# Attention B of a hybrid block: two small scalings moved from VectorE to ScalarE, and the next group's weight chunk converted later in the step

## The chip, the cores and the metric

One core of one Trainium2 chip runs the whole kernel. The metric is the device time in microseconds. The kernel before was timed three times: 1567.02, 1569.10 and 1569.83, median 1569.1.

## The reference, cut to what matters

The block computes attention A (32 heads of 16, 8 key groups, not causal), a mixture feed-forward, attention B, and the same feed-forward again, over 1024 tokens of width 512. Attention B is the part that matters here:

```
q, k, v = x @ w_q, x @ w_k, x @ w_v        # w = (4-bit integer - 8) * scale per 128 rows
q, k    = rope(q), rope(k)                 # 32 query heads, 8 key/value heads, head width 128
scores  = q @ k.T / sqrt(128), causal
attn    = softmax(scores)
out     = (attn @ v) @ w_o
```

## The kernel before, in words

Attention B runs over 8 groups g (one key/value head and R = 4 query heads each) and, in each, over T = 8 tiles t of 128 tokens: 64 steps, u = 8 g + t. In a step head h has scores of 128 queries against n = 128 (t + 1) keys, so that steps grow with t. All products are made of fp16 halves (high and low), three matmuls for each product.

Each engine has its own program, and within an engine everything runs in the written order; semaphores tie the engines together. There is no planner: the order around the change is the order in the function `step` of each engine.

TensorE (L1519): keys of head 0, the projection of the next tile (L1438), keys of head 1, half of the output product of the tile two before, keys of head 2, the other half, keys of head 3, then `turn_b` (L1453: five transposes of the next tile's rotated q and k) and `values` (L1500: attention times v for the tile before). Keys of head 0 wait for the low halves of the turned q and k (`s_ql`) and for the third exponentials of the tile before; keys of head 2 and 3 wait for exponentials 0 and 1 (`s_eb`), whose banks they write. `turn_b` waits for the rotation on GpSimd (`s_rpa`) and for the low half of v (`s_vl`). `values` waits for the transposing DMAs of the tile before (`s_tp`).

VectorE (L1066): `low` of heads 2 and 3 of the tile before (L1036, it writes the low half of the normalised attention), with `maximum` of head 0 between them; `dequantise` of one weight chunk of the next group (L932: tiles 0 to 3 have one of 768 columns, tiles 4 to 7 one of 512); the rotation of the next tile (L999, L1010); maximum 1; `invert` for heads 0 and 1; the low half of v (L992); maximum 2; low of head 0; maximum 3; `turned` (L1041, low halves of q, then k); low of head 1; invert for heads 2 and 3; `add` (L1051); `context_low` (L1059). `maximum` reduces a head's scores to the negated row maximum `nmr` (L1021) and multiplies it by the group's factor into `nmb` (L1023). `invert` scales the row sums `den` (L1031) and takes the reciprocal (L1034) into `rden`.

ScalarE (L659): `exponentials` of head 0 and 1 (L672, with the row sum in `den`, which a second instruction reads out of the accumulator), `values` (L638, high half of v), `high` of head 0 and 1 (L680: attention times `rden`, high half), `high_part` (L596: the dequantised chunk copied to fp16, L600 or L602), `turned` (L643: high halves of q, L645, and k, L648), exponentials 2 and 3, `context_high` of the tile before (L651), high 2 and 3. The last group has no chunk to dequantise or copy.

GpSimd (L511): `rope_add` (L500) and `low_part` (L502: what the fp16 copy left out, L505 or L508). The SyncE queue (L447): the DMAs of the chunk three steps on, which wait for earlier dequantised and split chunks, and a transposing DMA for each head (L459), which waits for `low`.

Quoted, a part of ScalarE's step (L683 to L698):

```
                exponentials(0)
                exponentials(1)
                if not end:
                    values(u + 1, par if t < T - 1 else 1 - par, t2)
                high(0)
                high(1)
                if not last:
                    high_part(g + 1, t, 1 - par)
                if not end:
                    turned(u + 1, t2, par if t < T - 1 else 1 - par)
                exponentials(2)
                exponentials(3)
                if exists(*before(g, t, 1)):
                    context_high(*before(g, t, 1))
                high(2)
                high(3)
```

Of the kernel before, what the change touches and what calls it, by code (L numbers as in the profile page):

```python
# [7 lines left out]
P = 128  # L8
# [9 lines left out]
R = NH // G  # L18
# [62 lines left out]
def build(nc, x_d, wq_d, bq_d, wk_d, bk_d, wv_d, bv_d, wo_d, bo_d,  # L81
# [6 lines left out]
    with ExitStack() as ctx:  # L88
# [67 lines left out]
        with ExitStack() as mem:  # L156
            xTh, xTl = (scoped(mem, f"xT{c}", [P, KC, S], F16) for c in "hl")
            qTh, qTl = (scoped(mem, f"qT{c}", [P, 2, R, P], F16) for c in "hl")
            kTh, kTl = (scoped(mem, f"kT{c}", [P, S + P], F16) for c in "hl")
            vh, vl = (scoped(mem, f"v{c}", [P, T + 2, P], F16) for c in "hl")  # L160
            cTh, cTl = (scoped(mem, f"cT{c}", [P, R, P], F16) for c in "hl")
            nmr = scoped(mem, "nmr", [P, R])
            nmb = scoped(mem, "nmb", [P, R])
            den = scoped(mem, "den", [P, R])
            rden = scoped(mem, "rden", [P, R])
            scoped(mem, "gap", [P, P])
            wh, wl = (scoped(mem, f"w{c}", [P, 2, KC, BW], F16) for c in "hl")
            woh, wol = (scoped(mem, f"wo{c}", [P, 2, R, D], F16) for c in "hl")
            st = scoped(mem, "st", [P, STAGES, BW])
            scale = scoped(mem, "scale", [P, 2, BW])  # L170
            cos = scoped(mem, "cosines", [P, T, HALF_D])
            sin = scoped(mem, "sines", [P, T, HALF_D])
            mask = scoped(mem, "mask", [P, P], BF16)
            ftmp = scoped(mem, "ftmp", [P, 4 * D + 16 * T + 8 * P + 4 * NE])
            hl = scoped(mem, "hl", [P, R, 2 * S], F16)
            hlT0 = scoped(mem, "hlT0", [P, R, 2 * (T - 1), P], F16)
            hlT1 = scoped(mem, "hlT1", [P, R, 2 * T, P], F16)
# [166 lines left out]
        def exists(g, t):  # L344

            return not (isinstance(g, int) and g < 0)
# [179 lines left out]
        def _(act):  # L526
# [132 lines left out]
            def step(g, t, par):  # L659

                u = g * T + t
                n = (t + 1) * P
                last = isinstance(g, int) and g == G - 1
                end = last and t == T - 1
                g2, t2 = after(g, t)

                def exponentials(h):
                    if exists(*before(g, t, 1)) is False:
                        act.wait_ge(s_nat[h], 64)
                        act.wait_ge(s_xh, 2 * T + 2 * h + 2)  # L670
                    act.wait_ge(s_nb, u * R + h + 1)
                    nc.scalar.activation(pr[:, h, 0:n], flat(2 * (h % 2), n), ACT.Exp, bias=nmb[:, h:h + 1],  # L672
                                         scale=factor[:, par, 0:1], accum_out=den[:, h:h + 1]).then_inc(s_eb, 1)

                def high(h):
                    if h % 2 == 0:
                        act.wait_ge(s_rd, u * 2 + h // 2 + 1)
                    if exists(*before(g, t, 1)):
                        act.wait_ge(s_tp[h], u * 16)
                    nc.scalar.activation(hl[:, h, 0:n], pr[:, h, 0:n], ACT.Copy,  # L680
                                         scale=rden[:, h:h + 1]).then_inc(s_hi, 1)

                exponentials(0)  # L683
                exponentials(1)
                if not end:
                    values(u + 1, par if t < T - 1 else 1 - par, t2)
                high(0)
                high(1)
                if not last:
                    high_part(g + 1, t, 1 - par)  # L690
                if not end:
                    turned(u + 1, t2, par if t < T - 1 else 1 - par)
                exponentials(2)
                exponentials(3)
                if exists(*before(g, t, 1)):
                    context_high(*before(g, t, 1))
                high(2)
                high(3)  # L698
# [21 lines left out]
        def _(dve):  # L720
# [295 lines left out]
                                               ALU.mult, ALU.mult).then_inc(s_rope, 1)  # L1016
                nc.vector.tensor_tensor(o[:, :, HALF_D:], rotary_in()[:, :, 0:HALF_D], sn, ALU.mult).then_inc(s_rope, 1)  # L1017

            def maximum(u, h, n, par):
                dve.wait_ge(s_sc, u * R + h + 1)  # L1020
                nc.vector.tensor_reduce(nmr[:, h:h + 1], flat(2 * (h % 2), n), AX.X, ALU.max, negate=True).then_inc(s_mxb, 1)  # L1021
                dve.wait_ge(s_mxb, u * R + h + 1)
                nc.vector.tensor_scalar(nmb[:, h:h + 1], nmr[:, h:h + 1], factor[:, par, 0:1], None,  # L1023
                                        ALU.mult).then_inc(s_nb, 1)

            def group_factor(g, par):
                nc.vector.tensor_copy(factor[:, par, :], factors[:, ds(g, 1), :].rearrange("p o a -> p (o a)")).then_inc(s_fcr, 1)

            def invert(u, a):
                dve.wait_ge(s_eb, u * R + 2 * a + 2)  # L1030
                nc.vector.tensor_scalar(rden[:, 2 * a:2 * a + 2], den[:, 2 * a:2 * a + 2], 1.0 / PSCALE, None,  # L1031
                                        ALU.mult).then_inc(s_dn, 1)
                dve.wait_ge(s_dn, u * 2 + a + 1)
                nc.vector.reciprocal(rden[:, 2 * a:2 * a + 2], rden[:, 2 * a:2 * a + 2]).then_inc(s_rd, 1)  # L1034

            def low(u, h, n):  # L1036
                dve.wait_ge(s_hi, u * R + h + 1)
# [28 lines left out]
            def step(g, t, par):  # L1066

                u = g * T + t
                n = (t + 1) * P
                last = isinstance(g, int) and g == G - 1  # L1070
                end = last and t == T - 1
                g2, t2 = after(g, t)
                one, two = before(g, t, 1), before(g, t, 2)
                if exists(*one):
                    low(u - 1, 2, (one[1] + 1) * P)
                if t == 0:
                    dve.wait_ge(s_fcr, g + 1)
                maximum(u, 0, n, par)
                if exists(*one):
                    low(u - 1, 3, (one[1] + 1) * P)  # L1080
                if not last:
                    dequantise(g + 1, t)
                if not end:
                    rope_cos(u + 1, t2)
                    rope_sin(t2)
                maximum(u, 1, n, par)
                invert(u, 0)
                if not end:
                    values_low(u + 1, par if t < T - 1 else 1 - par, t2)
                maximum(u, 2, n, par)  # L1090
                low(u, 0, n)
                maximum(u, 3, n, par)
                if not end:
                    turned(u + 1, t2, par if t < T - 1 else 1 - par)
                else:
                    final_statistics(0, 1)
                low(u, 1, n)
                invert(u, 1)
                if exists(*two):
                    add(u - 2, two[1], par if t >= 2 else 1 - par)  # L1100
                if exists(*one):
                    context_low(*one)
                if t == T - 1 and not last:
                    group_factor(g + 1, 1 - par)
# [482 lines left out]
```

## Time and profile before

| | |
|---|---|
| median of three runs | 1569.1 us |
| the profiled execution's own time | 1571.05 us |
| its span | 1569.2 us |
| TensorE clock over the span | 0.97 of full speed |
| steps of attention B | from 614 us to 1514 us of the span, 64 of them |
| instructions | 23528 |

The span is the time from the first to the last instruction of the program. Times of events are microseconds from the span's start. A row of the timeline gives start, duration, engine, line, operation and what is written from what; brackets at its end give how long the engine stood idle before it and whom it then waited for. TensorE's rows show start times well, but its ends are modelled. A row that groups instructions gives their count, their busy time, the mean of one in ns, and the idle time before them with its releasers.

### The profile page before, as it was taken

Reading aid. Unit: us, or ns where it says so; the run is one execution under the profiler, and the core shown is the slowest. Engines: PE = TensorE matmul, PEld = TensorE weight load, DVE = VectorE, ACT = ScalarE, POOL = GpSimd, SP = SyncE. Lnnn points to the kernel's source line nnn. Section 1 sums busy time; section 2 is a strip of 40 time slices with the busy share of each in tenths; the row PEclk is TensorE's granted clock in tenths of the full one; section 3 lists DMA queues with packets and bytes.
Section 4 is the critical chain, followed back from the end, with each engine's and each line's share of the span. In section 5 each row is a group of like instructions: output and inputs, shape, how many; then the busy total and the mean of one; then the engine's idle time right before and its main releaser. Section 6 shows DMA issues by size and latency. Waiting matters only on the chain.

```text
span 1569.2 us, 23528 instructions
## 1 busy us (share of the span) xinstructions
PE 1469.0 (94%) x7932; PEld 698.8 (45%) x7932; DVE 1237.7 (79%) x2583; ACT 868.9 (55%) x1468; POOL 237.6 (15%) x174
## 2 busy tenths in 40 slices
PE   5779999999999997899999999998999999999988
PEld 3412333333333354455555555554555555555534
DVE  4288888888886388787897887887887888878873
ACT  2205767676778324565665665664665665646630
POOL 2002000000000132221212212212212212211020
PEclk9957999999999998999999999999999999999989
DMA  3894000000000233566576575675684674653621
GB/s 97 150 143 134 1 1 0 0 0 0 0 0 11 64 94 98 105 140 144 121 137 139 120 150 127 129 147 120 128 160 111 141 145 110 134 96 67 115 54 54
DMA packets 352234, 144.64 MB, mean 92 GB/s; under 512 B 314680, under 2 KB 324408, under 8 KB 352128
## 3 DMA queue, kind: packets, MB, share of 16 engines
q1 hardware_dynamic: 352144, 143.48, 43.8%
q8 instruction: 52, 0.85, 0.2%
q14 instruction: 38, 0.31, 0.1%
HBM read 59.64 MB, written 6.19 MB: 42 GB/s over the span
## 4 chain that ended last, share of the span: by engine, by line
PE 73%; DVE 14%; ACT 6%; DMA 3%; issue 3%; SPq 0%; POOL 0%; DVEq 0%; ACTq 0%
PE ps L1433 9%; PE ps L1215 9%; PE ps L1435 9%; PE ps L1434 9%; PE ps L1268 7%; PE ps L1254 7%; PE ps L1395 4%; PE ps L1514 3%; PE ps L1516 3%; PE ps L1515 3%; ACT hl L680 2%; DVE hl L1038 2%; PE ps L1358 2%; DMA scratch<-pieces 2%; PE ps L1458 2%
## 5 line engine op out<-in xcount | busy, mean ns | idle before, releaser
L672 ACT ACTIVATE x<-ps,nmb,factor 128x128 f32<-128x128 f32 (+7 forms) x256 | 211.6, 832 | 290.9 <-DVE nmb L1023 290.9
L823 DVE TENSOR_REDUCE mx<-ps 128x1 f32<-128x512 f32 x512 | 326.4, 686 | 52.8 <-PE ps L1215 49.4
L581 ACT ACTIVATE proj<-ps 128x1024 f32<-128x1024 f32 x256 | 248.4, 1021 | 105.7 <-PE ps L1254 104.8
L1215 PE MATMUL ps<-ks,qs 96*128 (+1 forms) x512 | 200.1, 414 | 16.3 <-DVE mx L823 8.5
L1038 DVE SCALAR_TENSOR_TENSOR hl<-x,rden,hl 128x128 f16<-128x128 f32 (+7 forms) x256 | 208.3, 814 | 4.6 <-ACT hl L680 4.3
L680 ACT ACTIVATE hl<-x,rden 128x128 f16<-128x128 f32 (+7 forms) x256 | 184.1, 767 | 23.2 <-DVE rden L1034 22.5
L1021 DVE TENSOR_REDUCE nmr<-ps 128x1 f32<-128x128 f32 (+7 forms) x256 | 191.9, 750 | 0.0
L500 POOL TENSOR_TENSOR tmp<-tmp 128x640 f32<-128x640 f32 x64 | 98.4, 1538 | 532.1 <-DVE tmp L1017 532.1
L1433 PE MATMUL ps<-wh,xTh 128*128 128x256 f16 (+1 forms) x512 | 167.6, 327 | 0.0
L1434 PE MATMUL ps<-wl,xTh 128*128 128x256 f16 (+1 forms) x512 | 167.5, 327 | 0.0
L1435 PE MATMUL ps<-wh,xTl 128*128 128x256 f16 (+1 forms) x512 | 167.4, 327 | 0.0
L1433 PE MATMUL ps<-kTh,qTh 128*128 128x512 f16 (+3 forms) x384 | 125.8, 328 | 35.5 <-DVE kTl L1048 22.9
L1254 PE MATMUL ps<-qs,ks 99*128 (+1 forms) x512 | 153.0, 384 | 1.1 <-ACT proj L581 0.8
L1268 PE MATMUL ps<-proj,vcur 128*32 128x512 f32 x1024 | 137.2, 608 | 0.6 <-ACT proj L581 0.6
L1215 PEld LDWEIGHTS ps<-ks,qs 96*128 (+1 forms) x512 | 45.1, 97 | 192.8 <-DVE mx L823 138.3
L1434 PE MATMUL ps<-kTl,qTh 128*128 128x512 f16 (+3 forms) x384 | 125.5, 327 | 0.0
L1435 PE MATMUL ps<-kTh,qTl 128*128 128x512 f16 (+3 forms) x384 | 124.5, 326 | 0.0
L1514 PE MATMUL ps<-hlT,vh 128*128 128x512 f16 x288 | 110.5, 384 | 7.4 <-DMA hlT<-hl 6.9
L1516 PE MATMUL ps<-hlT,vh 128*128 128x512 f16 x288 | 110.4, 383 | 0.0
L1515 PE MATMUL ps<-hlT,vl 128*128 128x512 f16 x288 | 110.4, 383 | 0.0
L1433 PE MATMUL ps<-woh,cTh 128*128 128x512 f16 x256 | 97.5, 381 | 2.0 <-DVE cTl L1062 2.0
L1435 PE MATMUL ps<-woh,cTl 128*128 128x512 f16 x256 | 97.8, 382 | 0.0
(155 smaller groups left out, 2149.6 us busy)
## 6 DMA issues: line engine op xcount, KB each, us to landing
scale<-sp_n SPq DMA_DIRECT2D x32, 384.0 KB, 4.3
st<-in_L_attn_b_qw_q_dram SPq DMA_DIRECT2D x32, 256.0 KB, 2.8
st<-in_L_attn_b_qw_o_dram SPq DMA_DIRECT2D x32, 256.0 KB, 3.0
scale<-so_n SPq DMA_DIRECT2D x32, 256.0 KB, 3.6
qs<-scratch SPq DMA_DIRECT2D x24, 256.0 KB, 8.4
hlT<-hl SPq DMA_TRANSPOSE x256, 3.5
scratch<-pieces SPq DMA_DIRECT2D x5, 768.0 KB, 13.4
xnat<-attn_a_hidden_state_dram SPq DMA_DIRECT2D x8, 256.0 KB, 4.8
```

What stands on the lines that cost most here:

```text
L581: nc.scalar.activation(pbuf[:, e % 4, :].rearrange("p (b n) -> p b n", b=2), ps[:, b:b + 2, :], ACT.Exp, scale=float(HD) ** -0.5).then_inc ...
L672: nc.scalar.activation(pr[:, h, 0:n], flat(2 * (h % 2), n), ACT.Exp, bias=nmb[:, h:h + 1], scale=factor[:, par, 0:1], accum_out=den[:, h:h ...
L680: nc.scalar.activation(hl[:, h, 0:n], pr[:, h, 0:n], ACT.Copy, scale=rden[:, h:h + 1]).then_inc(s_hi, 1)
L823: nc.vector.tensor_reduce(mx[:, f, k // 2, k % 2:k % 2 + 1], ps[:, bank(k), :], AX.X, ALU.max).then_inc(s_mx, 1)
L1021: nc.vector.tensor_reduce(nmr[:, h:h + 1], flat(2 * (h % 2), n), AX.X, ALU.max, negate=True).then_inc(s_mxb, 1)
L1038: nc.vector.scalar_tensor_tensor(hl[:, h, n:2 * n], pr[:, h, 0:n], rden[:, h:h + 1], hl[:, h, 0:n], ALU.mult, ALU.subtract).then_inc(s_lo, 1)
L1215: mm(ps[:, bank, :], qs[0:STACK, ds(g * R + h, 1), f * HALF + qt * P:f * HALF + (qt + 1) * P], ks[0:STACK, ds(g, 1), kh * HALF:(kh + 1) * ...
L1254: ins = mm(ps[:, 4 + 2 * r + j, :], ks[0:STACK + NEG, ds(g, 1), kt * P:(kt + 1) * P], qs[0:STACK + NEG, ds(g * R + 2 * r + j, 1), f * HALF ...
L1268: ins = mm(ps[VW * j:VW * j + VW, 3, :], vcur[:, kt, :], pbuf[:, 2 * (kt % 2) + j // 2, (j % 2) * HALF:(j % 2 + 1) * HALF], start=(kt == 0 ...
L1433: mm(out, lh, rh, start=(start and i == 0), stop=False)
L1434: mm(out, lh, rl, start=False, stop=False)
L1435: ins = mm(out, ll, rh, start=False, stop=(stop and i == len(left) - 1))
```

## The change

It does three things. The multiplication of the negated maximum by the factor (`nmb`) leaves `maximum` on VectorE and becomes an ACTIVATE Copy with a per-partition scale on ScalarE, in front of each exponential. The scaling of the row sums leaves `invert` and becomes an ACTIVATE Copy with a constant scale on ScalarE, after exponentials 1 and 3, into a new tensor `sums_scaled` that takes its room from the unused `gap`; the reciprocal on VectorE reads it. And `high_part` moves from between high(1) and turned to behind exponentials 3 (and the second sums), in front of `context_high`.

```diff
@@ -163,7 +163,8 @@
             rden = scoped(mem, "rden", [P, R])
-            scoped(mem, "gap", [P, P])
+            sums_scaled = scoped(mem, "sums_scaled", [P, R])
+            scoped(mem, "gap", [P, P - R])
...
@@ -668,9 +669,17 @@
+                    act.wait_ge(s_mxb, u * R + h + 1)
+                    nc.scalar.activation(nmb[:, h:h + 1], nmr[:, h:h + 1], ACT.Copy,
+                                         scale=factor[:, par, 0:1]).then_inc(s_nb, 1)
                     act.wait_ge(s_nb, u * R + h + 1)
                     nc.scalar.activation(pr[:, h, 0:n], flat(2 * (h % 2), n), ACT.Exp, bias=nmb[:, h:h + 1],
                                          scale=factor[:, par, 0:1], accum_out=den[:, h:h + 1]).then_inc(s_eb, 1)
+
+                def sums(a):
+                    act.wait_ge(s_eb, u * R + 2 * a + 2)
+                    nc.scalar.activation(sums_scaled[:, 2 * a:2 * a + 2], den[:, 2 * a:2 * a + 2], ACT.Copy,
+                                         scale=1.0 / PSCALE).then_inc(s_dn, 1)
...
@@ -682,16 +691,18 @@
                 exponentials(0)
                 exponentials(1)
+                sums(0)
                 if not end:
                     values(u + 1, par if t < T - 1 else 1 - par, t2)
                 high(0)
                 high(1)
-                if not last:
-                    high_part(g + 1, t, 1 - par)
                 if not end:
                     turned(u + 1, t2, par if t < T - 1 else 1 - par)
                 exponentials(2)
                 exponentials(3)
+                sums(1)
+                if not last:
+                    high_part(g + 1, t, 1 - par)
                 if exists(*before(g, t, 1)):
                     context_high(*before(g, t, 1))
                 high(2)
...
@@ -1016,22 +1027,16 @@
-            def maximum(u, h, n, par):
+            def maximum(u, h, n):
                 dve.wait_ge(s_sc, u * R + h + 1)
                 nc.vector.tensor_reduce(nmr[:, h:h + 1], flat(2 * (h % 2), n), AX.X, ALU.max, negate=True).then_inc(s_mxb, 1)
-                dve.wait_ge(s_mxb, u * R + h + 1)
-                nc.vector.tensor_scalar(nmb[:, h:h + 1], nmr[:, h:h + 1], factor[:, par, 0:1], None,
-                                        ALU.mult).then_inc(s_nb, 1)
...
             def invert(u, a):
-                dve.wait_ge(s_eb, u * R + 2 * a + 2)
-                nc.vector.tensor_scalar(rden[:, 2 * a:2 * a + 2], den[:, 2 * a:2 * a + 2], 1.0 / PSCALE, None,
-                                        ALU.mult).then_inc(s_dn, 1)
                 dve.wait_ge(s_dn, u * 2 + a + 1)
-                nc.vector.reciprocal(rden[:, 2 * a:2 * a + 2], rden[:, 2 * a:2 * a + 2]).then_inc(s_rd, 1)
+                nc.vector.reciprocal(rden[:, 2 * a:2 * a + 2], sums_scaled[:, 2 * a:2 * a + 2]).then_inc(s_rd, 1)
```

## Rows read from the trace of the kernel before

**Rows 1.** The page, busy time by engine, and its group of the exponentials.

```profile
PE 1469.0 (94%) x7932; PEld 698.8 (45%) x7932; DVE 1237.7 (79%) x2583; ACT 868.9 (55%) x1468; POOL 237.6 (15%) x174
...
L672 ACT ACTIVATE x<-ps,nmb,factor 128x128 f32<-128x128 f32 (+7 forms) x256 | 211.6, 832 | 290.9 <-DVE nmb L1023 290.9
```

**Rows 2.** One group's stretch: length, then PE, PEld, DVE, ACT, POOL busy, clock, DMA.

```profile
960.46:1071.35 110.89, 105.89 (x613) 57.71 (x612) 94.06 (x201) 66.15 (x136) 23.45 (x16) 1.00 0.64 133
```

**Rows 3.** Timeline of TensorE, group 3, where tiles 2, 3 and 4 begin.

```profile
971.70 0.34 PE L1433 MATMUL ps<-kTh,qTh 128*128 128x384 f16 x1 [1.58 <-DVE kTl L1048]
...
983.40 0.39 PE L1433 MATMUL ps<-kTh,qTh 128*128 128x512 f16 x1 [1.02 <-DVE kTl L1048]
...
995.71 0.39 PE L1433 MATMUL ps<-kTh,qTh 128*128 128x512 f16 x1 [0.34 <-DVE kTl L1048]
```

**Rows 4.** Timeline of group 3, tile 7: exponentials 1 read out, keys of head 3.

```profile
1048.98 0.19 ACT L672 ACTIVATION_READ_ACCUMULATOR x<-ps,nmb,factor 128x1 f32 x1
...
1049.46 0.38 PE L1433 MATMUL ps<-kTh,qTh 128*128 128x512 f16 x1
```

**Rows 5.** Timeline of ScalarE and VectorE, group 3, tiles 2, 3 and 7.

```profile
981.68 0.57 ACT L645 ACTIVATE qTh<-ps 128x512 f16<-128x512 f32 x1
...
983.62 0.60 ACT L656 ACTIVATE cTh<-ps 128x512 f16<-128x512 f32 x1
...
985.35 0.61 DVE L1038 SCALAR_TENSOR_TENSOR hl<-x,rden,hl 128x384 f16<-128x384 f32 x1
985.87 0.68 DVE L1021 TENSOR_REDUCE nmr<-ps 128x1 f32<-128x512 f32 x1
...
986.72 0.61 DVE L1038 SCALAR_TENSOR_TENSOR hl<-x,rden,hl 128x384 f16<-128x384 f32 x1
...
993.26 0.83 ACT L600 ACTIVATE wh<-st 128x768 f16<-128x768 f32 x1
994.00 0.58 ACT L645 ACTIVATE qTh<-ps 128x512 f16<-128x512 f32 x1
...
1052.23 0.57 ACT L645 ACTIVATE qTh<-ps 128x512 f16<-128x512 f32 x1
```

**Rows 6.** Timeline of tile 1's chunk and turned q in group 3; last group's keys.

```profile
969.25 0.82 ACT L600 ACTIVATE wh<-st 128x768 f16<-128x768 f32 x1
969.98 0.57 ACT L645 ACTIVATE qTh<-ps 128x512 f16<-128x512 f32 x1
...
1415.13 0.34 PE L1433 MATMUL ps<-kTh,qTh 128*128 128x384 f16 x1 [1.13 <-DVE kTl L1048]
```

**Rows 7.** Groups by line and shape, ScalarE: count, busy us, mean ns, idle before.

```profile
L680 ACT ACTIVATE hl<-x,rden 128x1024 f16<-128x1024 f32 x32 | 34.9, 1140 | 2.3 <-DVE rden L1034 2.3
...
L680 ACT ACTIVATE hl<-x,rden 128x128 f16<-128x128 f32 x32 | 11.0, 392 | 5.9 <-DVE rden L1034 5.9
...
L606 ACT ACTIVATE rts<-rts 128x2 f32<-128x2 f32 x8 | 1.6, 203 | 12.1 <-DVE rts L909 11.7
```

**Rows 8.** Timeline of group 3, tile 1: maximum 1, nmb and the exponential.

```profile
966.48 0.41 DVE L1021 TENSOR_REDUCE nmr<-ps 128x1 f32<-128x256 f32 x1
966.93 0.21 DVE L1023 TENSOR_SCALAR nmb<-nmr,factor 128x1 f32<-128x1 f32 x1
...
967.18 0.57 ACT L672 ACTIVATE x<-ps,nmb,factor 128x256 f32<-128x256 f32 x1 [3.60 <-DVE nmb L1023]
```

**Rows 9.** Timeline of VectorE's low and GpSimd's low_part, group 3, tile 0.

```profile
954.60 0.34 DVE L1038 SCALAR_TENSOR_TENSOR hl<-x,rden,hl 128x128 f16<-128x128 f32 x1
...
955.59 1.65 POOL L505 TENSOR_TENSOR wl<-st,wh 128x768 f16<-128x768 f32 x1 [1.76 <-ACT wh L600]
...
956.99 0.39 DVE L1038 SCALAR_TENSOR_TENSOR hl<-x,rden,hl 128x128 f16<-128x128 f32 x1
```

More of the change, by code:

```diff
@@ L1077, in step @@
                     dve.wait_ge(s_fcr, g + 1)
-                maximum(u, 0, n, par)
+                maximum(u, 0, n)
                 if exists(*one):
@@ L1085, in step @@
                     rope_sin(t2)
-                maximum(u, 1, n, par)
+                maximum(u, 1, n)
                 invert(u, 0)
@@ L1089, in step @@
                     values_low(u + 1, par if t < T - 1 else 1 - par, t2)
-                maximum(u, 2, n, par)
+                maximum(u, 2, n)
                 low(u, 0, n)
-                maximum(u, 3, n, par)
+                maximum(u, 3, n)
                 if not end:
```

## The prediction, made before the result

> **What bounds the kernel now.** I read the page's busy shares first: TensorE 94%, VectorE 79%, ScalarE 55% [rows 1]. The change touches only the 64 steps of attention B (8 groups of 8 tiles), so I cut out one group that repeats, from the first keys product of group 3's tile 1 to that of group 4's tile 1: 110.89 us, TensorE busy 105.89, granted clock 1.00 [rows 2]. The other groups but the last look alike, so one group times seven is the scale.
>
> Then TensorE's timeline for what it waits on. Where tiles 2, 3 and 4 begin, keys of head 0 wait for VectorE's kTl: idle 1.58, 1.02 and 0.34 us [rows 3]. From tile 4 on TensorE has no gap until the next group, whose tile 0 waits for the second exponentials and for transposes. But "no gap" is not "much slack": in tile 7 the accumulator read of the second exponentials starts at 1048.98 and takes 0.19, and the fourth head's keys, which wait for it, start at 1049.46 [rows 4]. Less about 0.06 us from a release to a matmul that is 0.2 us of slack; in tiles 1 to 6 I find 0.2 to 0.5.
>
> So two things matter: the chain to kTl (turned q and k on ScalarE, then on VectorE), and a **ring** through ScalarE and VectorE that brings one step's turned q to the next one's: exponentials 2 and 3, context_high, high(2), low(2), maximum 0, low(3), dequantise, rope, maximum 1, exponentials 1, rden, high(0), high(1), turned. In tile 2 it goes from 981.68 to 994.00, 12.32 us [rows 5]. TensorE's own step is 12.31 (983.40 to 995.71) [rows 3]. Ring and TensorE are equally long.
>
> **Part 1: the chunk behind the fourth exponentials.** In tile 1 high_part starts at 969.25 and holds turned until 969.98; the last group has no chunk, and its TensorE idles 1.13 us where group 3's idles 1.58 [rows 3, 6]: 0.45 less. So turned would start at 969.53; tiles 2 and 3 of the last group compare in the same way, with 0.5 and 0.3. By itself this is worth some 1.1 us a group, for the stalls of rows 3 can shrink but no more. Its DMAs: none is issued by it. SP's wait for the rounded chunk is three steps behind and clears; the transposes on the same queue land more than 2 us before they are needed, save in tile 0, where they end the wait now and their start does not move. POOL's low_part starts 0.08 us after high_part and so moves too (below).
>
> **Part 2: the tiny scalings.** Removed from VectorE in each step: four of L1023 and two of L1031. Where maximum 0 or 1 is followed by it, the next instruction comes 0.17 us after the maximum's end (985.87 + 0.68 to 986.72) [rows 5]; without it, it can start 0.08 before that end: 0.25 us of VectorE's queue each.
> Added to ScalarE: four nmb with a pointer scale, two sums with a constant one. The trace has no such ACTIVATE of one element. high() is the same operation from and to SBUF with a pointer scale: 392 ns for 128 elements, 1140 for 1024, slope 0.835, so 286 ns for one. Below stands the two-element one with constants, 203 ns; above, the 392 ns row itself [rows 7]. I take 286, the line through rows of the same form, and 190 to 200 for sums (the 0.83 us of the 768-element copy less 767 x 0.833 ns is 0.19) [rows 5].
> Each nmb is followed by an exponential that waits for it. ScalarE's instructions without a wait overlap by about 0.10 us (970.07 to 969.98) [rows 6]. With one, as VectorE's nmb shows, 0.04 us passes from end to start [rows 8]. So exponentials 2 and 3, which today start 0.10 before the end of what stands before them, will start 0.19 + 0.04 after it: **+0.33 us each**. Before exponentials 0 and 1 ScalarE is idle; today maximum's end 966.89 to exponential 967.18 is 0.29 [rows 8], then 0.04 + 0.286 + 0.04 = 0.37: +0.08.
> Here a rule is weighed. The rows above say that the whole 0.286 lies on the path, since the next instruction reads its result. The Trainium skill (Perfetto Trace Analysis, Optimizing Scalar/DVE Operations) gives about 93 ns of engine-busy time to a ScalarE access of SBUF. By it, an estimate, each of the two would cost 0.09 in place of 0.33 and the sum below would end some 5 us under the time before; but the page adds that it counts without the write acknowledgement, which a dependent instruction must await.
>
> **POOL's port.** When VectorE's low runs into low_part, it is held: POOL 955.59 + 1.65 = 957.24, low (128 elements) ends 957.38, that is 128/0.96 ns later, and takes 0.39 in place of 0.34 [rows 9]. The same shows in tiles 1 to 3, where today the hit is only 0.04 us because low begins 0.24 before POOL's end. After the move low_part starts at context_high's start + 0.17 and runs 1.64, while low(2) of the next step would start at + 1.25 and stream from + 1.45: held by 0.37 us in tiles 1 to 3; none later, where low_part is 1.15 us.
>
> **The ring, tile 2 to tile 3** [rows 5, 8], new less old:
> nmb 2 and 3: +0.66. sums(1), 0.04 + 0.19, and no overlap before it: +0.24. Chunk in front of context_high +0.74, gone in front of turned -0.74 (993.26 to 994.00). context_high to low(2), now 983.62 to 985.35 = 1.73 because VectorE's add and cTl stand between, then 0.60 + 0.04 + 0.61 = 1.25: -0.48. Port: +0.37. nmb 0 off VectorE: -0.25. VectorE's idle in front of rope: -0.10. Exponentials 1: +0.08. sums(0) in place of L1031: +0.05. Together **+0.57 us**: 12.9 in place of 12.32.
> The same sum with each tile's widths: tile 1 to 2 +0.3, 2 to 3 +0.6, 3 to 4 +1.0 (the chunk at the front of tile 4 is only 0.52 long, the one behind tile 3's exponentials 0.74), 4 to 5 +0.5, 5 to 6 +0.4, 6 to 7 0 (context_high then waits for TensorE, as today). Against today's turned starts (969.98, 994.00, 1052.23) [rows 5, 6] it stands at -0.45 in tile 1, -0.2 in tile 2, +0.4 in tile 3, +1.4, +1.9, +2.3, and +2.3 in tile 7. What TensorE meets is exponentials 1, which lie ahead of the old chunk: +2.3 + 0.5 - 0.2 of slack = **+2.6 us a group**. Tile 0 neither gains nor loses: its TensorE has 5 us of context products as cover, and the next group starts from zero again.
> Seven groups with a chunk: 7 x 2.6 = 18.2. The last group, without chunks and dequantising, has room for the scalings: +0.1. Sum **+18 us**. The profiled execution took 1571.05 (span 1569.2 and 1.85 around it), 1.95 over the median of 1569.1; so it would take 1589, and the median is forecast at **1587**.
>
> **Own range of this case.** Each 0.01 us of nmb or its wait counts three times in seven steps of seven groups, 1.5 us. nmb at 203 ns: -12; at 392: +16. Without the port: -7. Wait 0.10 instead of 0.04, five times a step: +15. From 1568 to 1603.
>
> **Rivals.**
> 1. Faster: ScalarE swallows the scalings. ScalarE idles 290.9 us in front of its exponentials [rows 1], VectorE is the fuller engine and gets back 256 nmb of 0.21 us [rows 8] and the 128 of L1031. Then only the chunk's move and VectorE's relief count: 1.1 to 1.3 us a group, 1560. Place: exponentials 2 and 3; it decides once nmb with its wait costs under about 0.2 us. For it: the stalls of rows 3 are real. Against it: the 290.9 us lie before exponentials 0 and 1, and 2 and 3 run back to back. The skill's same section holds that with VectorE saturated "offloading some work to Scalar (or even GPSIMD) may make sense"; by that rule this rival would win. Chance 0.15.
> 2. No change: tiny operations near 203 ns and no port hold: gains in tiles 1 to 3 meet losses in 4 to 7; 1569. Chance 0.08.
> 3. Slower still: ScalarE waits for its own result longer than VectorE does (0.10 and more); 1600. No row shows ScalarE waiting for itself. Chance 0.10.
> 4. It doesn't do what it says: sums_scaled is cut from the gap, so nothing behind it moves, and each removed instruction has one on ScalarE. Only if the chunk were waited for by something near would it differ; nothing is. Under 0.01, counted with 2.
>
> **The numbers.** The forecast has 0.67, the rest as above. The range, 1566 to 1600, leaves out rival 1's core and half of rival 3. A measurement of this kernel tells 0.2%, 3.1 us. Slower by more 0.76, within 0.09, faster 0.15.
>
> **What would show it.** nmb on ScalarE at 0.28 to 0.29 us, the exponential 0.04 after it; turned in tile 1 0.4 earlier, in tile 5 or later over 1 us later; idle on TensorE before the fourth head's keys in tiles 3 to 7, released by ScalarE's exponentials, where there is none; low(2) in tiles 1 to 3 stretched by 0.3 to 0.4 and ending with POOL; one group 113.5 in place of 110.9. If tiles 4 to 7 stay without a gap, the ring had slack that I did not see, and the forecast is wrong.

## The result and the profile after

The changed kernel takes **1592.9 us** (median of six runs, 1588.5 to 1594.8); the kernel before, on the same chip, 1568.3 us (six runs, 1566.5 to 1569.8). The ratio is 1.0147, 95% interval 1.0128 to 1.0166: 1.5% slower. Here and below the ratio is estimated from the runs of both kernels and is not the quotient of the two medians (1.0157). The forecast was 1587 us with a range of 1566 to 1600: side and range hold, and the median lies 6 us above the forecast.

The profiled execution took 1588.45 us, span 1586.7, so 17.4 us more than that of before; the forecast for it was 1589. That near hit is partly chance, as the accounts below show.

The profile page of the changed kernel: busy time and the groups that answer to [rows 1], then the keys products and the reciprocal:

```profile
PE 1476.0 (93%) x7932; PEld 694.6 (44%) x7932; DVE 1179.4 (74%) x2199; ACT 966.6 (61%) x1852; POOL 237.9 (15%) x174
...
L676 ACT ACTIVATE x<-ps,nmb,factor 128x128 f32<-128x128 f32 (+7 forms) x256 | 213.0, 832 | 8.5
L673 ACT ACTIVATE nmb<-nmr,factor 128x1 f32<-128x1 f32 x256 | 74.5, 291 | 233.3 <-DVE nmr L1032 233.3
...
L1438 PE MATMUL ps<-kTh,qTh 128*128 128x512 f16 (+3 forms) x384 | 125.9, 328 | 42.6 <-ACT x L676 29.8
...
L1039 DVE RECIPROCAL rden<-sums_scaled 128x2 f32<-128x2 f32 x128 | 21.2, 166 | 142.1 <-ACT sums_scaled L681 142.1
```

VectorE is 58 us less busy, ScalarE 98 us more, TensorE's share falls by a point. ScalarE still idles 233.3 us, now in front of nmb, of the 290.9 that looked like room [rows 1]. And the keys products now wait for ScalarE's exponentials above all (29.8 of 42.6 us), where before it was kTl:

```profile
L1433 PE MATMUL ps<-kTh,qTh 128*128 128x512 f16 (+3 forms) x384 | 125.8, 328 | 35.5 <-DVE kTl L1048 22.9
```

The chain of work that ended last, as shares of the span by engine, says the same of the whole kernel. Before:

```profile
PE 73%; DVE 14%; ACT 6%; DMA 3%; issue 3%; SPq 0%; POOL 0%; DVEq 0%; ACTq 0%
```

and with the change, in which ScalarE and VectorE stand on it for 45% of the span and not for 20%:

```profile
PE 47%; ACT 24%; DVE 21%; DMA 4%; issue 3%; SPq 1%; POOL 0%; ACTq 0%; DVEq 0%
```

One group that repeats and three tiles 0, in the view of windows (length, then PE, PEld, DVE, ACT and POOL busy, granted clock, DMA share, GB/s), answering to [rows 2]:

```profile
965.68:1079.19 113.51, 107.35 (x613) 57.20 (x612) 86.83 (x153) 78.45 (x184) 23.49 (x16) 1.00 0.62 130
951.70:967.40 15.70, 13.67 (x75) 6.89 (x74) 8.06 (x20) 7.09 (x23) 3.17 (x2) 0.89 0.59 127
1066.80:1080.90 14.10, 12.01 (x75) 6.52 (x74) 8.05 (x20) 7.10 (x23) 3.17 (x2) 1.00 0.66 141
1180.30:1196.10 15.80, 13.73 (x75) 6.94 (x74) 8.10 (x20) 7.09 (x23) 3.18 (x2) 0.89 0.56 126
```

The group takes 113.51 us, where 113.5 was forecast and 110.89 stood before [rows 2]. Tiles 0 of groups 3 and 5 take 1.6 us longer than that of group 4, at a mean granted clock of 0.89. TensorE's timeline inside the tile 0 of group 3 shows what that is:

```profile
956.75 0.23 PE L1438 MATMUL ps<-kTh,qTh 128*128 128x128 f16 x1 [1.05 <-ACT x L676]
957.57 0.63 PE L1463 MATMUL ps<-ident,tmp 128*128 128x128 f32 x4 [0.42 <-DVE vl L1007]
...
958.87 0.58 PE L1519 MATMUL ps<-hlT,vh 128*128 128x512 f16 x1 [0.56 <-DMA hlT<-hl]
959.25 0.63 PE L1520 MATMUL ps<-hlT,vl 128*128 128x512 f16 x1
959.67 0.63 PE L1521 MATMUL ps<-hlT,vh 128*128 128x512 f16 x1
...
962.45 0.38 PE L1519 MATMUL ps<-hlT,vh 128*128 128x512 f16 x1
962.66 0.38 PE L1520 MATMUL ps<-hlT,vl 128*128 128x512 f16 x1
```

After three gaps of 1.05, 0.42 and 0.56 us the products start 0.42 us apart and later 0.21: the granted clock is 0.5 for 3.4 us from 958.8 on, the lower of the two levels, 1.2 in place of 2.4 GHz. The profile has such stretches in tile 0 of groups 3, 5 and 7; that of before has none in groups 1 to 7, although its gaps in that tile are of like size (1.02, 0.69 and 0.17 in group 3).

TensorE's gaps in the rest of group 3, answering to [rows 3, 4]. In tiles 2 to 5 the fourth head's keys wait (985.16, 997.99, 1011.44, 1025.46); at 988.64 it is keys of head 0 in tile 3, released by the third exponentials:

```profile
976.56 0.32 PE L1438 MATMUL ps<-kTh,qTh 128*128 128x384 f16 x1 [1.17 <-DVE kTl L1053]
985.16 0.34 PE L1438 MATMUL ps<-kTh,qTh 128*128 128x384 f16 x1 [0.32 <-ACT x L676]
988.64 0.38 PE L1438 MATMUL ps<-kTh,qTh 128*128 128x512 f16 x1 [0.63 <-ACT x L676]
997.99 0.39 PE L1438 MATMUL ps<-kTh,qTh 128*128 128x512 f16 x1 [0.59 <-ACT x L676]
...
1011.44 0.39 PE L1438 MATMUL ps<-kTh,qTh 128*128 128x512 f16 x1 [0.57 <-ACT x L676]
...
1025.46 0.39 PE L1438 MATMUL ps<-kTh,qTh 128*128 128x512 f16 x1 [0.25 <-ACT x L676]
```

ScalarE, VectorE and GpSimd between turned q of tile 1 and tile 2 in the same group, answering to [rows 5, 6, 8, 9]:

```profile
974.78 0.60 ACT L646 ACTIVATE qTh<-ps 128x512 f16<-128x512 f32 x1 [0.27 <-PE ps L1463]
...
975.43 0.29 ACT L673 ACTIVATE nmb<-nmr,factor 128x1 f32<-128x1 f32 x1
975.76 0.57 ACT L676 ACTIVATE x<-ps,nmb,factor 128x256 f32<-128x256 f32 x1
...
976.23 0.19 ACT L676 ACTIVATION_READ_ACCUMULATOR x<-ps,nmb,factor 128x1 f32 x1
976.32 0.28 ACT L673 ACTIVATE nmb<-nmr,factor 128x1 f32<-128x1 f32 x1
...
976.63 0.57 ACT L676 ACTIVATE x<-ps,nmb,factor 128x256 f32<-128x256 f32 x1
...
977.10 0.19 ACT L676 ACTIVATION_READ_ACCUMULATOR x<-ps,nmb,factor 128x1 f32 x1
...
977.32 0.20 ACT L681 ACTIVATE sums_scaled<-den 128x2 f32<-128x2 f32 x1
...
977.43 0.83 ACT L601 ACTIVATE wh<-st 128x768 f16<-128x768 f32 x1
...
978.34 1.64 POOL L506 TENSOR_TENSOR wl<-st,wh 128x768 f16<-128x768 f32 x1 [4.94 <-ACT wh L601]
...
979.38 0.88 DVE L1043 SCALAR_TENSOR_TENSOR hl<-x,rden,hl 128x256 f16<-128x256 f32 x1
...
986.75 0.60 ACT L646 ACTIVATE qTh<-ps 128x512 f16<-128x512 f32 x1
```

nmb takes 0.28 to 0.29 us, the exponential starts 0.04 after its end (975.43 + 0.29 to 975.76), and the sums start 0.03 after the accumulator read's end. GpSimd's low_part ends at 979.98; the low half of head 2 that ran into it ends at 980.26, 0.28 us later, which is about what its 256 elements take (by the same operation's 0.34 us for 128 elements and 0.88 for 640, an estimate of 1.05 ns an element), and takes 0.88 us where one of its shape next to it takes 0.47 to 0.48.

### The profile page after: what moved, and what is told of

It reads as the page before. It is cut to its first block, busy times and chain, and to the rows that moved or that the text cites. A ratio compares the mean times of both kernels' runs of the same rounds, so it can differ in the third digit from the quotient of the medians.

```text
span 1586.7 us, 23528 instructions
## 1 busy us (share of the span) xinstructions
PE 1476.0 (93%) x7932; PEld 694.6 (44%) x7932; DVE 1179.4 (74%) x2199; ACT 966.6 (61%) x1852; POOL 237.9 (15%) x174
## 4 chain that ended last, share of the span: by engine, by line
PE 47%; ACT 24%; DVE 21%; DMA 4%; issue 3%; SPq 1%; POOL 0%; ACTq 0%; DVEq 0%
ACT x L676 9%; PE ps L1220 9%; PE ps L1273 8%; PE ps L1259 7%; ACT hl L689 6%; DVE nmr L1032 5%; DVE hl L1043 4%; PE ps L1400 3%; DMA hlT<-hl 2%; DVE tmp L1014 2%; PE ps L1438 2%; PE ps L1440 2%; PE ps L1439 2%; ACT nmb L673 2%; DVE st L951 2%
## 5 line engine op out<-in xcount | busy, mean ns | idle before, releaser
L1043 DVE SCALAR_TENSOR_TENSOR hl<-x,rden,hl 128x128 f16<-128x128 f32 (+7 forms) x256 | 216.8, 847 | 5.9 <-ACT hl L689 4.7
L673 ACT ACTIVATE nmb<-nmr,factor 128x1 f32<-128x1 f32 x256 | 74.5, 291 | 233.3 <-DVE nmr L1032 233.3
L1032 DVE TENSOR_REDUCE nmr<-ps 128x1 f32<-128x128 f32 (+7 forms) x256 | 191.2, 747 | 0.0
L1438 PE MATMUL ps<-kTh,qTh 128*128 128x512 f16 (+3 forms) x384 | 125.9, 328 | 42.6 <-ACT x L676 29.8
L1039 DVE RECIPROCAL rden<-sums_scaled 128x2 f32<-128x2 f32 x128 | 21.2, 166 | 142.1 <-ACT sums_scaled L681 142.1
```

The costliest lines, as they stand in the source:

```text
L1043: nc.vector.scalar_tensor_tensor(hl[:, h, n:2 * n], pr[:, h, 0:n], rden[:, h:h + 1], hl[:, h, 0:n], ALU.mult, ALU.subtract).then_inc(s_lo, 1)
L1438: mm(out, lh, rh, start=(start and i == 0), stop=False)
```

## The experiments

Each run changes the attention B steps alone. "Tiles 1 to 7" below is group 3 from the first maximum of tile 1 to the first of the next group, read from the same view of windows in each run's profile; before has 96.80 us there and the changed kernel 99.38, and groups 1, 2 and 4 to 6 agree with group 3 within 0.04 in each of the two; group 0 does not (below). Each ratio is against the kernel before on the same chip. The runs were made on four chips, on which the median of the kernel before was 1568.4 to 1569.8 us, so a difference between medians of two runs is uncertain by about that much.

**1 and 2. Each part alone.** The chunk moved, all scalings on VectorE (the sums go to `sums_scaled` there):

```diff
                 high(0)
                 high(1)
-                if not last:
-                    high_part(g + 1, t, 1 - par)
...
                 exponentials(3)
+                if not last:
+                    high_part(g + 1, t, 1 - par)
```

> The chunk moved behind the fourth exponentials, all scalings left on VectorE. Ring theory: turned in tile 1 starts 0.45 us earlier, the idle time before keys of head 0 shrinks in tiles 2 to 4, and low_part's hold of low(2) (0.37 us in tiles 1 to 3) gives part of it back: 0.7 to 1.1 us a group, so 1561 to 1563. Rival (the move itself is what costs, through GpSimd's port or a later context_high): at least 1575.

The scalings moved, the chunk where it was (the diff is shortened: waits and semaphores are left out):

```diff
 def exponentials(h):
+    nc.scalar.activation(nmb[:, h:h + 1], nmr[:, h:h + 1], ACT.Copy, scale=factor[:, par, 0:1])
...
                 exponentials(1)
+                sums(0)
...
                 exponentials(3)
+                sums(1)
```

> The six scalings on ScalarE, the chunk left in front of turned. Ring theory: two nmb at +0.33 us, exponentials 1 at +0.08, sums +0.3, less 0.25 for VectorE; 1.9 us a group over before, 13 us, plus a few us if TensorE's clock drops in tile 0 as it did in three groups of the changed kernel: 1580 to 1588. Rival (ScalarE's idle time swallows the scalings): 1565 to 1570.

The chunk alone: 1568.7 us, ratio 0.9978 (0.9951 to 1.0005). The scalings alone: 1584.0 us, ratio 1.0083 (1.0060 to 1.0107). Windows of the chunk alone, tile 0 and tiles 1 to 7 of group 3:

```profile
945.85:961.63 15.78, 13.93 (x76) 7.02 (x75) 9.40 (x26) 5.51 (x17) 3.17 (x2) 0.89 0.67 131
961.63:1057.65 96.02, 93.86 (x540) 50.89 (x539) 85.24 (x177) 60.92 (x119) 20.31 (x14) 1.00 0.64 133
```

and of the scalings alone:

```profile
954.81:968.90 14.09, 12.05 (x75) 6.55 (x74) 8.13 (x21) 6.98 (x23) 3.18 (x2) 1.00 0.70 142
968.90:1067.54 98.64, 94.65 (x541) 50.82 (x540) 77.20 (x136) 71.12 (x161) 20.28 (x14) 1.00 0.62 130
```

In tiles 1 to 7 the chunk's move gains 0.78 us, the scalings cost 1.84, and both together cost 2.58, not 1.06. So the same move that helps alone costs 0.74 once the scalings are in: the ring then has no slack left to hide what the move brings with it. What that is, run 5 below shows: without GpSimd's low_part, whose hold of low(2) comes with the move, both together take 98.21 us, 0.43 less than the scalings alone (in run 2 low(2) is not held: 0.47 us). The scalings are the loss. The chunk alone missed its forecast of 1561 to 1563: its 5 us of gain in tiles 1 to 7 (seven groups at 0.78 is 5.5) are there, and three stretches at half clock in tile 0 (15.78 us in place of 14.13) take them back.

**3 and 4. Which scalings.** In both, the chunk is moved and the sums are on ScalarE; run 3 puts nmb of heads 2 and 3 back on VectorE, run 4 those of heads 0 and 1 (`on_scalar` is [0, 1] in run 3 and [2, 3] in run 4; waits and semaphores are left out).

```diff
 def exponentials(h):
+    if h in on_scalar:
         nc.scalar.activation(nmb[:, h:h + 1], ...)
...
 def maximum(u, h, n, par):
+    if h not in on_scalar:
+        nc.vector.tensor_scalar(nmb[:, h:h + 1], nmr[:, h:h + 1], factor[:, par, 0:1], None, ALU.mult)
```

> The changed kernel with nmb of heads 2 and 3 back on VectorE; nmb 0 and 1 and the sums stay on ScalarE. Ring theory: the two that stood back to back between exponentials are gone, 2 x 0.33 us of ring in each step: a group is 109.8 in place of 113.5, the kernel 1564 to 1567. Rival (every scaling costs the same, wherever it stands): half of the change's 24.5 us is left, 1580.

> The changed kernel with nmb of heads 0 and 1 back on VectorE; nmb 2 and 3 and the sums stay on ScalarE. Ring theory: nothing of the loss goes, and VectorE's 0.25 us of relief before low(3) is lost: a group is 113.5 to 114.0, the kernel 1593 to 1600. Rival (every scaling costs the same): 1580.

Run 3 took 1573.6 us, ratio 1.0020 (1.0000 to 1.0040); run 4 took 1595.6, ratio 1.0157 (1.0108 to 1.0206). Group of nmb on ScalarE and tiles 1 to 7, run 3:

```profile
L674 ACT ACTIVATE nmb<-nmr,factor 128x1 f32<-128x1 f32 x128 | 37.7, 295 | 237.5 <-DVE nmr L1033 237.5
...
963.23:1059.76 96.53, 94.25 (x540) 50.88 (x539) 81.07 (x150) 68.02 (x147) 20.33 (x14) 1.00 0.63 132
```

and run 4:

```profile
L674 ACT ACTIVATE nmb<-nmr,factor 128x1 f32<-128x1 f32 x128 | 36.7, 287 | 0.0
...
970.87:1071.20 100.33, 95.30 (x541) 50.68 (x540) 81.78 (x149) 67.22 (x147) 20.34 (x14) 1.00 0.60 128
```

The same instruction of 0.29 us, 128 of each: where 237.5 us of idle time stand in front of it, tiles 1 to 7 take 0.51 us more than in run 1 (the sums included) and still 0.27 less than before; where none does, they take 4.31 more than in run 1 and 3.53 more than before. Heads 2 and 3 on ScalarE cost 2.85 us a group (99.38 less 96.53). With these there, heads 0 and 1 on ScalarE give back 0.95 (100.33 less 99.38): VectorE's queue, which the ring runs through as well, has two instructions less, though that this is the cause was argued and not tested by itself. What nmb of head 0 alone does on ScalarE was not measured. Run 3's median is above its forecast of 1564 to 1567 in the main for the same reason as run 1's: its profile has four stretches at half clock. Its group, 110.6 us where the clock is full (96.53 and 14.1), also missed the 109.8 of the forecast.

**5. The port.** The changed kernel, but GpSimd's low_part copies one element in groups 2 to 7 in place of its subtraction. Left out: the low halves of those groups' weights, whose tiles keep old values; TensorE's products are as many and as long.

```diff
             def low_part(g, c, par):
                 pool.wait_ge(s_wh, g * CHUNKS + c + 1)
+                if g >= 2:
+                    pool.tensor_copy(iota8[:, 0:1], iota8[:, 0:1]).then_inc(s_wlp, 1)
+                    return
```

> The changed kernel with GpSimd's low_part of groups 2 to 7 replaced by a copy of one element, so the low halves of those groups' weights keep old values. Port theory: low(2) of tiles 1 to 3 is no longer stretched (0.37 us each), a group is 112.4 in place of 113.5, 6 groups, 6 to 7 us: 1585 to 1587. Rival (the hold costs nothing on the path): 1592.

It took 1582.9 us, ratio 1.0071 (1.0051 to 1.0091). The low half that took 0.88 us in the changed kernel, and tiles 1 to 7:

```profile
980.68 0.48 DVE L1046 SCALAR_TENSOR_TENSOR hl<-x,rden,hl 128x256 f16<-128x256 f32 x1
...
968.74:1066.95 98.21, 95.23 (x541) 50.66 (x540) 77.60 (x136) 71.37 (x161) 12.05 (x14) 1.00 0.63 130
```

1.17 us a group go with GpSimd's operation, which is the port's three times 0.37 of the prediction. The steps of six groups are without it (those of groups 1 to 6, which convert the weights of groups 2 to 7), 7.0 us together. The median is 10 us under the changed kernel's, 3 more than that and 2 below its own forecast. The clock can account for the rest: over the whole span the mean granted clock of its ten runs is 0.973, of the changed kernel's six 0.970, an estimate of 5 us.

**6 to 8. Filling the gaps of tile 0.** Nine extra matmuls whose results nobody reads, in tile 0 of groups 1 to 7: five in front of the fourth head's keys, two in front of the transposes, two in front of `values`. In the changed kernel (6), the kernel before (7) and the one with the chunk alone moved (8).

```diff
+                fill(g, t, par, 5)
                 keys(g, t, 3, par)
+                fill(g, t, par, 2)
                 if not end:
                     turn_b(u + 1)
+                fill(g, t, par, 2)
                 if exists(*one):
                     values(*one, par if t >= 1 else 1 - par)
```

> The changed kernel with nine extra matmuls in tile 0 of groups 1 to 7, where TensorE waits for exponentials 1, for the low half of v and for the transposes; their result is overwritten. Clock theory: the 24.5 us of the change are 18 of ring and some 5 of half-clock stretches of 3.4 us in tile 0, which in the profile cost about 1.6 us in each of three groups; with the gaps filled they go, all groups take 113.5, and the time is 1586 to 1589. Rival (the missing 6 us come from elsewhere): 1592 to 1595.

> The kernel before with the same nine matmuls in tile 0. Its profile shows no half clock in groups 1 to 7, so clock theory: within 2 us of the kernel before. Rival (its runs too have such stretches, other than its profile): 2 to 4 us faster. If the matmuls get in the way: slower by up to 2 us.

> The chunk alone moved behind the fourth exponentials, with the same nine matmuls. Its profile without them has a group 0.7 us shorter in tiles 1 to 7 than before, and three half-clock stretches in tile 0. Clock theory: these go, and what is left is the ring's gain, 5 us under the kernel before: 1562 to 1565. Rival: as without them, 1568 to 1569.

Medians: 1588.5 us (ratio 1.0112, 1.0081 to 1.0143), 1575.9 (1.0041, 1.0022 to 1.0060) and 1570.2 (0.9987, 0.9964 to 1.0009). No stretch at half clock is left in groups 1 to 7 of any of the three profiles. But the filler was no neutral tool: tile 0 of the kernel before grew from 14.13 to 14.85 us, because `values` starts later, waiting for a transposing DMA:

```profile
957.15 0.38 PE L1515 MATMUL ps<-hlT,vh 128*128 128x512 f16 x1 [0.45 <-DMA hlT<-hl]
```

By the trace's landing times that DMA took 5.60 us from its issue here and 4.88 in the kernel before, and 5.62 in run 8; in run 6, with the same nine matmuls, it took 4.85 in group 3 and over 5.5 in groups 4 and 7 only. Why is open. Runs 7 and 8 carry the same burden, so their difference can be read: 5.7 us for the chunk's move. The forecasts of run 7 (within 2 us of before) and of run 8 (1562 to 1565) were wrong; that of run 6 held.

**9. The chunk elsewhere.** Scalings on VectorE, the chunk between exponentials 0 and 1, and on GpSimd low_part in front of rope_add, to keep low_part off VectorE's low halves.

```diff
                 exponentials(0)
+                if not last:
+                    high_part(g + 1, t, 1 - par)
                 exponentials(1)
...
+                if not last:
+                    low_part(g + 1, t, 1 - par)
                 if not (last and t == T - 1):
                     rope_add(g * T + t + 1)
-                if not last:
-                    low_part(g + 1, t, 1 - par)
```

> All scalings on VectorE; the chunk between exponentials 0 and 1, where ScalarE idles over 3 us, and on GpSimd low_part before rope_add, so that it ends before VectorE's low operations. Ring theory: the chunk leaves the ring altogether, tiles 1 to 3 look like those of the last group, which has none: 1.2 us a group less than before, 1560 to 1562 without half-clock stretches in tile 0, up to 1566 with them. Rival (the step was bound elsewhere, or rope_add comes late): 1568 or more.

It took 1579.0 us, ratio 1.0063 (1.0045 to 1.0081): a miss. Windows of tile 0 and tiles 1 to 7, then the timeline from low_part to the transposes in tile 0:

```profile
949.84:966.24 16.40, 13.76 (x76) 7.45 (x75) 10.35 (x26) 5.62 (x17) 3.12 (x2) 0.90 0.57 126
966.24:1062.62 96.38, 94.10 (x540) 51.08 (x539) 85.12 (x177) 62.26 (x119) 20.07 (x14) 1.00 0.63 132
```

```profile
953.39 1.64 POOL L506 TENSOR_TENSOR wl<-st,wh 128x768 f16<-128x768 f32 x1 [14.25 <-ACT wh L601]
954.99 1.53 POOL L501 TENSOR_TENSOR tmp<-tmp 128x640 f32<-128x640 f32 x1
955.03 1.51 DVE L1032 TENSOR_SCALAR sums_scaled<-den 128x2 f32<-128x2 f32 x1 [0.62 <-ACT x L673]
956.58 0.17 DVE L1035 RECIPROCAL rden<-sums_scaled 128x2 f32<-128x2 f32 x1
956.66 0.27 DVE L997 SCALAR_TENSOR_TENSOR vl<-ps,vh 128x128 f16<-128x128 f32 x1
...
957.08 1.30 PE L1459 MATMUL ps<-ident,tmp 128*128 128x128 f32 x5 [1.62 <-DVE vl L997]
```

Tiles 1 to 7 even gain 0.42 us. Tile 0 loses 2.3: rope_add stands behind 1.64 us of low_part and ends at 956.52. VectorE's scaling of the sums, two elements a partition, ends 0.02 after it: it is held for 1.51 us, and behind it on VectorE stands vl, for which the transposes wait 1.62 us in place of 0.69. The longer gap is followed by half clock, here in six of the seven groups 1 to 7. Why the expectation failed: it priced low_part's collision with the low halves and not rope_add's with what stands in front of vl.

**10 to 12. Five extra matmuls alone.** Only the five in front of the fourth head's keys, where TensorE waits for the second exponentials: 1.05 us by the row at 956.75, 1.2 if one counts from when the next matmul could have started, 0.21 behind the start of the last one (five take 1.08 us): with the chunk alone moved (10), in the kernel before (11) and in the changed kernel (12).

```diff
+                fill(g, t, par, 5)
                 keys(g, t, 3, par)
```

> The chunk alone moved, with five of the nine extra matmuls, those in front of the fourth head's keys in tile 0. With all nine the half-clock stretches went but the transposing DMAs of tile 0 took 0.8 us longer. If the four behind these keys did that, this one keeps the full clock and the short DMAs: 1563 to 1565. If any added matmuls do it: 1568 to 1570.

> The kernel before with the same five extra matmuls (results unused) in front of the fourth head's keys of tile 0 in groups 1 to 7, nothing else. It separates the two things in the run that has them together with the moved chunk (1564.8 us). Theory A, the matmuls and the ring are independent: the group loses only what the moved chunk gave, 0.7 to 0.8 us in tiles 1 to 7, so 7 x 0.75 = 5.3 us more than 1564.8: 1569 to 1571, no stretch at half clock in groups 1 to 7, tile 0 at 14.1 us, and the gain over the kernel before is the moved chunk's alone. Rival B: the matmuls are what gained, and this kernel too comes in at 1564 to 1566.

> The changed kernel with the five extra matmuls in front of the fourth head's keys of tile 0, without the four behind the transposes and in front of the values. Theory: the stretches at half clock in tile 0 are gone and nothing is added on the path (the stall that they fill is 1.2 us, they take 1.08), so the time is the changed kernel's less its three or more stretches of 1.6 us: 1584 to 1588, and the ring's 2.6 us a group stay (tiles 1 to 7 of group 3 at 99.4 us). Rival: the half clock needs the other gaps filled too; then it stays at 1590 to 1594 with half-clock stretches in the trace.

| | median, us | ratio to before (95%) | tile 0, us | tiles 1 to 7, us |
|---|---|---|---|---|
| 10, chunk moved | 1564.8 | 0.9975 (0.9963 to 0.9987) | 14.12 | 96.02 |
| 11, before | 1568.4 | 0.9991 (0.9973 to 1.0009) | 14.14 | 96.79 |
| 12, changed kernel | 1584.9 | 1.0106 (1.0076 to 1.0136) | 14.09 | 99.38 |

Tile 0 and tiles 1 to 7 of run 12, whose granted clock is 1.00 in both:

```profile
952.82:966.91 14.09, 13.11 (x80) 7.05 (x79) 8.08 (x21) 7.09 (x23) 3.18 (x2) 1.00 0.67 142
966.91:1066.29 99.38, 95.30 (x541) 50.66 (x540) 78.77 (x136) 71.35 (x161) 20.33 (x14) 1.00 0.64 129
```

Run 12's median is 8.0 us under the changed kernel's, by the two ratios (1.0147 and 1.0106) 6.4, and its ring is as it was. The clock of all runs, not of the profiled one alone, bears this out: over the span 0.969 to 0.971 was granted in the six runs of the changed kernel, 0.974 to 0.976 in the five of run 12. The difference of the means, 0.005 of 1590 us, is an estimate of 8 us. Run 11, a little under its forecast of 1569 to 1571, finds nothing to gain where the profile had no half clock in those tiles. Run 10 is faster than both kernels, by 0.25% over before: the moved chunk is what it has over run 11, 3.6 us by the medians and 2.5 by the ratios. That is less than the 5.4 of tiles 1 to 7 (4.6 in groups 1 to 6). Between the two profiles, 2.7 us apart, the gain in the groups is there, and 2.4 us are lost behind the last group's tile 7, in code that is the same; why is open.

## Why the prediction was right, and where its size was off

**The ring, right in place and size.** The steps of the prediction against group 3 of the profile, with the lateness of turned q counted from the first keys product of tile 1, where the prediction's group begins:

| step of the prediction | forecast | measured |
|---|---|---|
| nmb on ScalarE, wait behind it | 0.286, 0.04 us | 0.29, 0.04 us |
| sums on ScalarE | 0.190 to 0.200 us | 0.20 us |
| turned q, tiles 1, 2, 3 | -0.45, -0.2, +0.4 us | -0.42, -0.15, +0.42 us |
| turned q, tiles 4, 5, 6, 7 | +1.4, +1.9, +2.3, +2.3 us | +1.35, +1.78, +2.16, +2.09 us |
| port hold in tiles 1 to 3, together | 1.1 us a group | 1.17 us (run 5) |
| one group | +2.6 us | +2.62 us (tiles 1 to 7: +2.58) |

The seven groups were not all alike, though. Tiles 1 to 7 take 2.56 us more in each of groups 1 to 6 (15.35 together) but only 0.7 more in group 0, where they took 99.1 already before and not 96.8; with 0.3 in the last group that is 16.4 us in place of 18.3. Run 12, in which the half clock is gone, took 1584.9, 16.3 over the 1568.65 of before on its chip. Idle in front of the fourth head's keys came a tile earlier than I said, in tile 2, and had all but gone in tiles 6 and 7. One wait I did not name: keys of head 0 in tile 3 wait for the third exponentials and no longer for kTl.

**The term that was missing.** Nothing in the prediction stands for TensorE's clock in tile 0; "tile 0 neither gains nor loses" is the step that failed. The profile shows three stretches there, 1.6 to 1.7 us each, some 5 us together, and run 12 says 6 to 8 us for the medians. The profiled execution still came to 17.4 us over before's, since other parts went the other way. Summed up between the two profiles: attention B begins 5.0 us earlier (615.25 against 610.27), group 0 is 3.0 longer, tiles 0 of groups 1 to 7 are 5.45 longer, tiles 1 to 7 of groups 1 to 6 are 15.35 longer, the last group's tiles 0.3, and from its tile 7 to the end it is 1.7 shorter: 17.4. So the profile's 1588.45 lies near the forecast of 1589 because a loss that was missed and an earlier start that nobody forecast cancel; its median is 4.4 us above it, where before's was 2.7 below its own profiled execution.

Why the half clock comes is open in part. Filling 1.08 us of a 1.2 us gap removes it from the profiles of two kernels (runs 10 and 12; with four more matmuls runs 8 and 6), a longer gap (run 9) makes it frequent, so the gaps of tile 0 are a condition. They are no sufficient one: the scalings alone have gaps of 1.06, 0.42 and 0.55 us in tile 0 of group 3, the changed kernel's to 0.01, and no half clock there or in any of groups 1 to 7; the chunk alone has it in group 3 behind gaps of 1.01, 0.69 and 0.15 us, where before has 1.02, 0.69 and 0.17 and none; and the changed kernel has it in groups 3, 5 and 7 only. What decides is not shown, and how often the kernel before has such stretches outside its profile was not seen.

**The chunk by itself.** Forecast at 1.1 us a group, measured at 0.78. The gaps before head 0's keys went from 1.58, 1.02 and 0.34 us [rows 3] to 1.13, 0.58 and 0.37: tiles 2 and 3 gained as the last group had suggested, tile 4 nothing. The forecast of that gain left out the port hold, which the chunk's move brings by itself: in that run a low half of 256 elements takes 0.87 us.

**The rivals.** Rival 1 (ScalarE swallows the scalings) needed them to cost under 0.2 us where exponentials 2 and 3 stand; runs 3 and 4 show 0.29 and the loss just there. Run 3 is rival 1's own world cut down to heads 0 and 1, and even it is no faster than before, although its four stretches at half clock (6.6 us in the profile) hide a ring that is 0.27 us a group shorter. The rule behind it, that with VectorE saturated offloading to ScalarE may make sense (the Trainium skill, Perfetto Trace Analysis, Optimizing Scalar/DVE Operations), did not help here: VectorE lost 58 us of busy time and the kernel 24.6 us of time, for the receiving engine stood on the path. VectorE was 79% busy, so whether it counts as saturated is open. Rival 2 needed tiny operations near 0.20 us and no hold: nmb takes 0.29, and the hold is 1.17 us a group. Rival 3 needed a wait of 0.10 us behind ScalarE's own result: it is 0.04.

The instruction's 0.29 us agree with a page that the prediction had not used: the Trainium skill (ScalarE: Activation LUTs, Rules for kernel authors) budgets about 0.3 us per ACTIVATE whose bias is a pointer operand, and some 0.83 ns an element; here it is the scale that is a pointer. The 93 ns that it did weigh are no latency; by them, an estimate of the prediction, the kernel would have come out some 5 us faster than before.

## What to carry to other kernels

A small operation is priced by where its result is awaited, not by which engine is fuller: nmb of heads 0 and 1, behind an idle gap, costs 0.5 us a group at most, the same instruction between back-to-back exponentials 2.85. Before work is moved to an engine "with idle time", look at which of its instructions the idle time stands in front of, and follow the ring from one step's turned q to the next one's; if it is as long as the bounding engine's step, all that is put into it shows. And when two edits travel together, time each alone: here one was worth keeping once the clock held (run 10 against run 11), and in the ring that the other had filled up GpSimd's hold turned it into a loss.

## What the runs showed of the hardware

- **TensorE's clock can fall after short gaps.** Three gaps of 1.05, 0.42 and 0.56 us in one tile of 14 us were followed by 3.4 us at half clock and cost 1.6 us; 1.08 us of matmuls whose results nobody reads, in the first of them, took 6 to 8 us off the changed kernel. Equal gaps are not always followed by it (three of seven groups), and the matmuls bring something only where the stretches are: the kernel before kept its time (0.9991, 0.9973 to 1.0009).
- **GpSimd can hold VectorE until its operation ends.** VectorE's low half with two SBUF inputs, run into low_part, ends 0.28 us after GpSimd's end (0.88 us in place of 0.48 for 256 elements), as if it began to stream only then. The Trainium skill (SBUF — State Buffer, SBUF: two separate sides) calls the shared port pair an exclusive lock, taken also by a VectorE operation with two SBUF inputs; the trace agrees. I had not expected it of an operation with one SBUF input and two elements: L1032 in run 9 takes 1.51 us beside rope_add, and in run 1 at the same place 0.57, where its shape alone takes 0.16. In the kernel before it takes 0.57 there too (953.28), while nmb with its one element, in the midst of the same rope_add in run 1, keeps its 0.21. The same section of the Trainium skill names VectorE's two-port performance modes as well; whether the two-element form runs in one and the one-element form does not, no run here shows. The changed kernel has this scaling on ScalarE, and its transposes in tile 0 wait 0.42 us where before's wait 0.69: a place in which the scalings' move shortened a wait of TensorE, though the wait behind it grew (0.56 in place of 0.17) and tile 0 gained nothing (14.09 us in run 2, 14.13 before).
- **A transposing DMA can take 0.7 us longer** (5.60 and 5.62 in place of 4.88 and 4.89) with four more matmuls around the transposes on TensorE, in the kernel before and in the one with the chunk moved; five earlier ones alone leave it at 4.87 to 4.89 (runs 10 and 11). In the changed kernel the same matmuls left it at 4.85 in group 3, so they are not enough by themselves. Nothing here says why.
